# Transformer block in fp32 on one core: the opening rebuilt, weights on a second DMA queue, statistics of batch 0 on VectorE, FFN weight scaling moved into later tiles

## What is computed

```python
def _L0_attn_ref(x, W_qk, W_v, alibi_slope):
    scores = jnp.einsum('bqe,bke->bqk', x @ W_qk, x) * SCALE
    scores = scores + (kpos - qpos) * alibi_slope[0]
    scores = jnp.where(causal, scores, -jnp.inf)
    attn = jax.nn.softmax(scores, axis=-1)
    return jnp.einsum('bqk,bkd->bqd', attn, x @ W_v.T)
def _L0_ffn_ref(x, w_gate, w_up, w_down):   # weights are int32, times 1/127
    h = jax.nn.silu(jnp.einsum('bsd,hd->bsh', x, wg)) * jnp.einsum('bsd,hd->bsh', x, wu)
    return jnp.einsum('bsh,dh->bsd', h, wd)
x = x + _L0_attn_ref(_layernorm(x), W_qk, W_v, alibi_slope)
x = x + _L0_ffn_ref(_layernorm(x), w_gate, w_up, w_down)
```

## Time and profile before

| what | us |
|---|---|
| median of 3 runs | 145.16 (144.49 to 145.37) |
| the profiled execution, whole | 145.67 |
| its span, first to last instruction | 143.9 |
| outside the span (difference) | 1.77 |

### The profile page before, as it was taken

How to read it: one execution, slowest core, us unless ns; L and a number is a source line. 1 busy time by engine, 2 the same in 40 slices (tenths; PEclk the granted TensorE clock), 3 DMA queues, 4 the chain that set the end, 5 groups by cost and what they waited for, 6 DMA issues and landing times.

```text
span 143.9 us, 3450 instructions
## 1 busy us (share of the span) xinstructions
PE 122.8 (85%) x1215; PEld 91.9 (64%) x1215; DVE 120.7 (84%) x341; ACT 110.7 (77%) x251; POOL 97.6 (68%) x157
## 2 busy tenths in 40 slices
PE   0239658999999999999999998979998899999942
PEld 0028345867987769978779776657755656675541
DVE  0729989998697996969996969999879999988781
ACT  4034588999976999949999769985699978999830
POOL 6490769964993454992438943798999999646810
PEclk9999999999999999999999999999999999999995
DMA  4997000000000000000000000000000222022204
GB/s 129 221 244 190 0 0 2 7 2 0 5 0 0 5 0 2 5 0 0 0 5 0 5 0 2 2 5 0 5 0 0 77 77 66 12 73 77 77 0 146
DMA packets 9811, 5.18 MB, mean 36 GB/s; under 512 B 448, under 2 KB 9792, under 8 KB 9792
## 3 DMA queue, kind: packets, MB, share of 16 engines
q1 hardware_dynamic: 9792, 4.92, 12.2%
HBM read 2.82 MB, written 2.10 MB: 34 GB/s over the span
## 4 chain that ended last, share of the span: by engine, by line
PE 50%; DVE 23%; ACT 9%; POOL 7%; DMA 4%; issue 3%; SPq 2%; DVEq 0%
PE work_ps L556 7%; POOL hidden_lo L411 6%; PE attn_ps L571 5%; PE attn_ps L573 4%; PE attn_ps L572 4%; PE score_ps L504 4%; PE score_ps L506 4%; DVE probsT_lo L824 4%; PE score_ps L505 4%; DMA wd_int<-in_L_ffn_w_down_dram 4%; DVE biased L841 3%; PE score_ps L595 2%; PE score_ps L592 2%; DVE stats L726 2%; ACT silu L1069 2%
## 5 line engine op out<-in xcount | busy, mean ns | idle before, releaser
L571 PE MATMUL attn_ps<-v_hi,probsT_hi 128*128 128x128 f16 x144 | 25.8, 219 | 3.0 <-DVE xs L851 2.4
L824 DVE TENSOR_TENSOR probsT_lo<-work_ps,probsT_hi 128x512 f16<-128x512 f32 (+3 forms) x48 | 25.2, 552 | 3.5 <-ACT probsT_hi L1007 3.4
L1007 ACT CAST probsT_hi<-work_ps 128x512 f16<-128x512 f32 (+3 forms) x48 | 21.4, 484 | 7.7 <-PE work_ps L556 7.4
L992 ACT ACTIVATE probs<-biased,neg_max 128x128 f32<-128x128 f32 (+7 forms) x32 | 25.0, 783 | 1.9 <-DVE neg_max L841 1.9
L841 DVE CUSTOM_DVE_ANT_0 biased<-score_ps,bias,neg_score_scale 128x128 f32<-128x128 f32 (+7 forms) x32 | 25.8, 806 | 0.6 <-PE score_ps L506 0.6
L573 PE MATMUL attn_ps<-v_hi,probsT_lo 128*128 128x128 f16 x144 | 25.8, 219 | 0.0
L572 PE MATMUL attn_ps<-v_lo,probsT_hi 128*128 128x128 f16 x144 | 25.8, 219 | 0.0
L556 PE MATMUL work_ps<-ident,probs 128*128 128x128 f32 x144 | 21.4, 274 | 0.2 <-DVE probsT_lo L824 0.2
L411 POOL TENSOR_TENSOR hidden_lo<-hidden,hidden_hi 128x512 f16<-128x512 f32 x13 | 17.6, 1375 | 5.1 <-ACT hidden_hi L1075 5.1
L556 PEld LDWEIGHTS work_ps<-ident,probs 128*128 128x128 f32 x144 | 16.5, 141 | 3.2 <-DVE probsT_lo L824 0.5
L437 POOL TENSOR_TENSOR xT_lo<-whole,xT_hi 128x512 f16<-128x512 f32 x8 | 9.3, 1163 | 13.6 <-ACT whole L986 13.6
(11 more groups left out here) (135 smaller groups left out, 346.7 us busy)
## 6 DMA issues: line engine op xcount, KB each, us to landing
out_dram<-xs SPq DMA_DIRECT2D x7, 256.0 KB, 2.7
xs<-in_L_attn_x_dram SPq DMA_DIRECT2D x3, 512.0 KB, 7.4
xs<-in_L_attn_x_dram SPq DMA_DIRECT2D x2, 256.0 KB, 3.0
out_dram<-xs SPq DMA_DIRECT2D x2, 128.0 KB, 1.9
wgu_int<-in_L_ffn_w_gate_dram SPq DMA_DIRECT2D x1, 192.0 KB, 3.1
wgu_int<-in_L_ffn_w_up_dram SPq DMA_DIRECT2D x1, 192.0 KB, 3.4
wd_int<-in_L_ffn_w_down_dram SPq DMA_DIRECT2D x1, 192.0 KB, 5.1
wqk_in<-in_L_attn_W_qk_dram SPq DMA_DIRECT2D x1, 64.0 KB, 2.9
```

What stands on the lines that cost most here:

```text
L571: pe.matmul(attn_ps[:, 0:D], p_hi, v_j, start=(j == 0), stop=False)
L824: dve.tensor_tensor(probsT_lo[:, i % 2, cols], work_ps[:, bank, 0:n], probsT_hi[:, i % 2, cols], ALU.subtract).then_inc(work_emptied, 1)
L992: act.activation(probs[:, i % 2, 0:n], biased[:, i % 2, 0:n], ACT.Exp, bias=neg_max[:, i:i + 1], scale=-1.0, accum_out=prob_sum[:, i:i + 1 ...
L1007: act.copy(probsT_hi[:, i % 2, CW * h:CW * h + n], work_ps[:, bank, 0:n]).then_inc(probsT_hi_ready, 1)
```

## The change

- **Loads.** The weights and the slope are issued by ACT instead of SP, ahead of everything else on ACT. SP issues batch 0 and then waits for `w_down` before it issues batches 1 to 3. ACT waits for gate and up alone before it casts those.
- **Statistics of batch 0.** POOL's `norm(0)` is gone. DVE takes the attention maxima first, then the statistics, then computes the variances of all eight tiles in seven small steps (`first_variances`); POOL only raises them to the power -0.5, one half at a time; DVE normalises both halves (`normalise_first`).
- **Attention weights.** ACT makes the scaled and high parts, POOL the low ones; DVE did both.
- **Order of the opening.** xT0, q0, xT1, v0, q1, probabilities of tile 0, v1, instead of xT0, xT1, q0, q1, v0, v1, probabilities. PE turns gate and up before xT0 and down after it. The statistics of batch 1 are taken in two groups of four. `norm(1)` on POOL is done half by half.
- **Parts of batch 1**, made during batch 0, move from steps 1 to 6 to steps 3 to 7; for its first halves of xT and q DVE makes the low part from PSUM, and ACT makes no whole copy.
- **FFN weights.** The maxima go to steps 5 and 6 of batch 0 (DVE). The exponents, powers and scales go to steps 1, 2 and 3 of batch 1 (DVE, with a transpose and a spreading matmul on PE in the ring). The scaling goes from ACT to POOL, during batch 2, ahead of `norm(4)`. The high parts go to steps 0 and 1 of batch 3 (ACT), the low parts to POOL in batch 3, ahead of `norm(5)`.

The rest of the diff replaces expressions for indices and counts by a table (`ring`) with the same meaning. The core of the diff:

```diff
+    opening = [("xT", 0), ("q", 0), ("xT", 1), ("v", 0), ("q", 1), ("P", 0), ("v", 1)]
...
+    def parts_at(b, i):
+
+        if b == 0:
+            return {3: [("xT", 0)], 4: [("xT", 1), ("q", 0)], 5: [("q", 1)], 6: [("v", 0)], 7: [("v", 1)]}.get(i, [])
+        return prologue[:HALVES if b == B - 1 else None][i - 1:i] if i else []
...
+    FFN_W = 1
...
+    def by_pool(key):
+
+        return key[0] in ("xT", "q") and (key[1] > 1 or key[1:] == (1, 1))
...
-            sp.dma_start(wqk_in[:, :], w_qk).then_inc(attn_w_loaded, 16)
...
-            sp.dma_start(wgu_int[:, 0:HB, :], w_gate.rearrange("(j p) d -> p j d", p=P)).then_inc(ffn_w_loaded, 16)
...
-            sp.dma_start(wd_int[:, :], w_down).then_inc(ffn_w_loaded, 16)
...
+            sp.wait_ge(wd_loaded, 16)
             for b in range(1, B):
                 sp.dma_start(xs[:, TB * b:TB * (b + 1), :], xv[b]).then_inc(x_loaded[b], 16)
...
-            norm(0)
...
+            first_rstd()
+
+            def attention_weight_low(k):
+                pool.wait_ge(attn_w_scaled, k + 1)
+                pool.wait_ge(attn_w_hi_ready, k + 1)
+                part = (wqk, wvT)[k]
+                pool.tensor_tensor(part[:, 1, :], wtmp[:, k, :], part[:, 0, :], ALU.subtract).then_inc(attn_w_ready, 1)
...
+            attention_weight_low(0)
...
-            norm(1)
...
-            pool.wait_ge(ffn_w_hi_ready, 1)
-            pool.tensor_tensor(wguT[:, 1, :, :], wguT_f[:, :, :], wguT[:, 0, :, :], ALU.subtract).then_inc(ffn_w_ready, 1)
-            pool.tensor_tensor(wdT[:, 1, :, :].rearrange("p a n -> p (a n)"), wdT_f[:, :],
-                               wdT[:, 0, :, :].rearrange("p a n -> p (a n)"), ALU.subtract).then_inc(ffn_w_ready, 1)
...
+            attention_weight_low(1)
+            slopes(slice(0, CW))
+
+            mean_step, var_step = moments(1)
+            for h in range(HALVES):
+                inverse_deviation(1, slice(CT * h, CT * h + CT), var_step)
+                centre(1, h, mean_step)
+                scale(1, h)
...
+            def ffn_weights_scaled():
+                pool.wait_ge(int_scale_ready, 1)
+                pool.wait_ge(ffn_w_copied, 3)
+                for k, w in enumerate((gu_f, d_f)):
+                    pool.tensor_tensor(w, w, int_scale[:, k:k + 1].broadcast_to([P, w.shape[1]]), ALU.mult)\
+                        .then_inc(ffn_w_scaled, 1)
+
+            def ffn_weights_low():
+                for k, (w, hi, lo) in enumerate(((gu_f, gu_hi, gu_lo), (d_f, d_hi, d_lo))):
+                    pool.wait_ge(ffn_w_hi_ready, k + 1)
+                    pool.tensor_tensor(lo, w, hi, ALU.subtract).then_inc(ffn_w_ready, 1)
...
             for b in range(B - 1):
                 nxt = (b + 1) % 2
-                for part in prologue:
-                    if by_pool(part):
-                        split_low(b + 1, nxt, *part)
+                for kind, h in prologue:
+                    if by_pool((kind, b + 1, h)):
+                        split_low(b + 1, nxt, kind, h)
+                if b == FFN_W + 1:
+                    ffn_weights_scaled()
                 norm(b + 2)
             for part in prologue[:HALVES]:
                 split_low(B, B % 2, *part)
+            ffn_weights_low()
             norm(B + 1)
...
+                    if (b, i) == (FFN_W, 1):
+                        pe.wait_ge(w_max_ready, 2)
+                        fill(("wmax", 0, 0), lambda ps: turn_maxima(1, ps))
+                    if (b, i) == (FFN_W, 2):
+                        taken(("wmax", 0, 0))
+                        fill(("wpow", 0, 0), lambda ps: spread_powers(1, ps))
...
+            keep_busy(4)
...
+            spread_powers(0, attn_ps[:, 256:258]).then_inc(w_pow_spread, 1)
+            pe.wait_ge(ffn_w_float, 1)
+            for j in range(2 * HB):
+                m = pe.transpose(gate_up_w_ps[j // HB][:, P * (j % HB):P * (j % HB + 1)], wgu_in[:, j, :], ident[:, :])
+                if j % HB == HB - 1:
+                    m.then_inc(ffn_w_turned, 1)
+            prologue_part(0, 0, "xT", 0)
             pe.wait_ge(ffn_w_float, 2)
-            for j in range(2 * HB):
-                pe.transpose(gate_up_w_ps[j // HB][:, P * (j % HB):P * (j % HB + 1)], wgu_in[:, j, :], ident[:, :])
...
+            keep_busy(2)
             pe.wait_ge(attn_w_ready, 1)
...
+            prologue_part(0, 0, "q", 0)
+            prologue_part(0, 0, "xT", 1)
...
+            pe.wait_ge(attn_w_ready, 2)
+            prologue_part(0, 0, "v", 0)
...
+            def first_variances():
+                stat = stats[:, apart(0), :, :]
+                dve.tensor_tensor(mean_dif[:, :], stat[:, :, 1], stat[:, :, 4], ALU.subtract)
+                dve.tensor_tensor(square_sum[:, :], stat[:, :, 2], stat[:, :, 5], ALU.add)
+                link(dve.tensor_tensor(mean_sum[:, :], stat[:, :, 1], stat[:, :, 4], ALU.add))
+                dve.tensor_tensor(dif_sq[:, :], mean_dif[:, :], mean_dif[:, :], ALU.mult)
+                link(dve.tensor_scalar(within_eps[:, :], square_sum[:, :], 1.0 / D, EPS, ALU.mult, ALU.add))
+                dve.scalar_tensor_tensor(var_eps[:, :], dif_sq[:, :], 0.25, within_eps[:, :], ALU.mult, ALU.add)\
+                   .then_inc(first_var_ready, 1)
+                link(dve.tensor_scalar(mean[:, apart(0), :], mean_sum[:, :], 0.5, None, ALU.mult))
+
+            def normalise_first(h):
+                dve.wait_ge(first_rstd_ready, h + 1)
+                for j in range(CT * h, CT * h + CT):
+                    dve.tensor_scalar(xn[:, j, :], xs[:, j, :], mean[:, 1, j:j + 1], rstd[:, 1, j:j + 1],
+                                      ALU.subtract, ALU.mult).then_inc(first_tokens_ready, 1)
...
+                    if b == FFN_W - 1 and i in (5, 6):
+                        ffn_maxima(i - 5)
+                    if b == FFN_W and i in (1, 2, 3):
+                        (ffn_exponents, ffn_powers, ffn_scales)[i - 1]()
...
-
+                    if b == FFN_W + 2 and i in (0, 1):
+                        ffn_weights_high(i)
...
+            act.dma_start(wqk_in[:, :], w_qk).then_inc(attn_w_loaded, 16)
+            act.dma_start(wv_in[:, :], w_v).then_inc(attn_w_loaded, 16)
+            act.dma_start(wgu_int[:, 0:HB, :], w_gate.rearrange("(j p) d -> p j d", p=P)).then_inc(gu_loaded, 16)
+            act.dma_start(wgu_int[:, HB:2 * HB, :], w_up.rearrange("(j p) d -> p j d", p=P)).then_inc(gu_loaded, 16)
+            act.dma_start(wd_int[:, :], w_down).then_inc(wd_loaded, 16)
...
+            act.wait_ge(gu_loaded, 32)
             act.copy(wgu_in[:, :, :], wgu_int[:, :, :]).then_inc(ffn_w_float, 1)
+            act.wait_ge(wd_loaded, 16)
...
+            def attention_weight(k, source):
+                act.activation(wtmp[:, k, :], source, ACT.Copy, scale=wpow_inv[:, k:k + 1]).then_inc(attn_w_scaled, 1)
+                act.activation((wqk, wvT)[k][:, 0, :], source, ACT.Copy, scale=wpow_inv[:, k:k + 1])\
+                   .then_inc(attn_w_hi_ready, 1)
...
+            def ffn_weights_high(k):
+                act.wait_ge(ffn_w_scaled, k + 1)
+                hi, f = ((gu_hi, gu_f), (d_hi, d_f))[k]
+                act.copy(hi, f).then_inc(ffn_w_hi_ready, 1)
```

522 lines of the change are left out of this document (247 added, 275 removed).

## The result

The changed kernel takes 153.79 us (median of four runs, 152.74 to 154.94) against 144.86 for the kernel before (144.49 to 145.37). The ratio is 1.063, its 95% interval 1.056 to 1.069: it is slower by 6.3%, where I had forecast no measurable difference. The profiled execution has a span of 152.6 us, 8.7 more than that of before.

What follows compares the result with a forecast made beforehand. It took the opening as a chain of waits through the last FFN load, and POOL's list as the path in the last third. Terms -4.3 + 1.3 + 0.4 + 0.1 + 2.8 = +0.3 gave median 145.5 us, range 142.8 to 147.8.

Steps and rivals of the forecast that it cites:

- the opening: Up to DVE's step 0 of batch 0: earlier normalising and less DVE work gain 4.3 us, bounds 3.0 to 5.3.
- batch 0: Added DVE work and a PE stall in step 4 lengthen this batch by 1.3 us, bounds -0.5 to +2.5.
- batch 1: DVE's FFN steps in steps 1 to 3, with 0.45 us of room, add 0.4 us, bounds 0 to 1.2.
- the closing: POOL's FFN low parts ahead of norm(5) push its list, delaying PE's down: +2.8 us, bounds 1.5 to 3.3.
- W_v was put at 3.8: Opening loads: W_v, now second in its queue, was to arrive at about 3.8 us; before, it was awaited until 5.81.
- both hops together: Opening: two hops through PE and ACT for q0 were to show about 1 us more of waiting.
- The stall of PE in step 4: Batch 0: PE was to stand some 2.4 us before batch 1's first scores, awaiting DVE's low part of q0.
- `norm(1)` ends well ahead of its use: POOL's norm of batch 1 was to finish in time, as batch 1's first xT is wanted only in step 3.
- Batch 2: Two FFN scalings on POOL, which runs about 2 us ahead of PE, add 0.1 us, bounds 0 to 0.5.
- My second rival: PE's stall in batch 0, step 4 lowers its clock, costing 1.5 us more: 147.0 us; chance 0.16.
- POOL's list not the path: First rival: POOL's list does not set the closing, which costs 0.6 instead of 2.8 us: 143.3 us; chance 0.27.
- The late second half of the tokens: Third rival: this half lands at 6.8 and delays all variances; opening gains 2.8 us: 147.0 us; chance 0.12.

Runs made afterwards that it cites:

- run 3: Changed kernel with batch 1's parts one per step, steps 2 to 7 of batch 0, instead of two in step 4; 154.06 us, ratio 1.065.
- run 5: Changed kernel with batch 1's statistics ahead of the first scores, its parts in steps 1 to 6, split by POOL; 153.05 us, ratio 1.059.
- run 7: Changed kernel with run 5's order, DVE's FFN work in opening gaps and batch 1 step 5, POOL and ACT FFN work re-placed; 146.81 us, ratio 1.019.
- run 4: Changed kernel with DVE's FFN exponents in step 7 of batch 0, powers and scales in step 7 of batch 1; 154.12 us, ratio 1.064.
- run 1: Changed kernel with POOL's FFN low parts and scalings and ACT's FFN high casts one batch earlier; 149.15 us, ratio 1.030.
- run 6: Kernel before with only POOL's two FFN low parts moved from behind norm(1) to ahead of the closing's norm; 149.65 us, ratio 1.035.
- run 11: Kernel before, unchanged, profiled once more in one execution; 143.98 us.
- run 9: Run 8's kernel with the second half of the first tokens normalised by POOL instead of DVE; 146.08 us, ratio 1.013.
- run 8: Run 7's kernel with POOL's FFN scalings behind norm(2) instead of norm(3); 145.41 us, ratio 1.007.
- run 10: Run 8's kernel with eleven more filling transposes on PE in the opening; 144.04 us, ratio 0.996.

## Why the prediction was wrong

The measured sum is 8.4 us above the forecast one: 2.2 of them lie in the opening, 1.2 in batch 0, 2.0 in batch 1 and 3.1 in the closing. The step that failed most is the closing's: a delay of POOL's list was priced at its own length. Even with every term at its upper bound (-3.0 + 2.5 + 1.2 + 0.5 + 3.3 = 4.5) the forecast would have ended at 149.7 us.

**The opening: -4.3 forecast, -2.1 in the two profiles, -1.0 against the opening that two further executions show.** Three steps failed. First, W_v was put at 3.8 and came at 4.62, which with the small steps makes the first normalising 0.9 us late. Second, the stretch from there to step 0 was to shrink by 1.0 us and grew by 0.4, to 21.87 - 9.66 = 12.21 (11.85 before). I had taken 3.7 us of DVE's work out of it as if DVE alone set its length. From the first normalising to xT's low part DVE needed 12.21 - 9.66 = 2.55 us where before it was 15.52 - 12.12 = 3.40. DVE's work went, but PE's transposes (1.06 us, where they took 0.72 before) and ACT's copy (DVE idle 0.92 before 12.21) took its place, so 0.85 was gained, though some 2.5 us of work had left this part; I had allowed 1.0 for both hops together. From there to step 0 the changed kernel needs 9.66 us and the kernel before 8.45, 1.2 more: the second half's normalising took 1.96 us and not 1.12, beside three spans of POOL. Third, the base: the chain of one execution, whose last load was late, was taken for the program's own, and the wait for that late load was the very thing the change removes.

**Batch 0: +1.3 forecast, +2.5 measured, which is the upper bound that I gave.** The stall of PE in step 4 is there, but 1.82 of its 2.4 us wait for a free bank and only 0.61 for q's low part, so its length is right in part by luck. And the step "`norm(1)` ends well ahead of its use" was wrong in what it left unsaid: it ends in time for the late places only. Runs 3 and 5 show it. As the statistics of batch 1 moved behind the first scores, POOL's norm begins 0.6 us before step 0 (21.25 against 21.87) and not 5.1 (18.89 against 23.97 before), and PE cannot use its waits of steps 0 to 2. An earlier norm gave back 1.1 us; run 7, with the two maxima taken off DVE there as well, gave back the rest and more (19.89).

**Batch 1: +0.4 forecast, +2.4 measured; bounds 0 to 1.2, so outside them.** The term was mis-sized: "Steps 1, 2 and 3 get 0.7, 0.45 and 0.65 us on DVE". They got, from DVE's timeline of the changed kernel, 1.3 (47.81 to 49.11), 0.45 and 1.44 (54.39 to 55.83), since `wpow_diag` took 0.90 us instead of 0.22 and `gu_square` 0.94 instead of 0.16. And the room of 0.45 us in step 1, which I read from a single pair of rows, was no room in steps that are DVE's to begin with: the three steps grew by 1.3, 0.5 and 1.0 us. Run 4 gave back 1.1 of the 2.4; run 7, with almost all of it outside the batch, gave back all.

**Batch 2: +0.1 forecast, 0 measured.** Right; POOL's two scalings are hidden.

**The closing: +2.8 forecast, +5.9 measured.** The mechanism was right, and runs 1 and 6 isolate it: POOL's list is the path, and the work ahead of `norm(5)` moves it all. Measured from DVE's step 7, the norm starts 3.0 us later (97.19 - 104.66 against 91.47 - 101.89), which is my term. Mis-sized is what comes behind, which I had put at nothing. The rows of the kernel before that answer to the later ones are

```profile
110.74 2.73 POOL L411 TENSOR_TENSOR hidden_lo<-hidden,hidden_hi 128x512 f16<-128x512 f32 x2
...
113.53 0.23 PE L688 MATMUL attn_ps<-wdT,hidden_hi 128*128 128x128 f16 x1 [0.44 <-POOL hidden_lo L411]
...
115.08 0.75 DVE L941 SCALAR_TENSOR_TENSOR xs<-attn_ps,ffn_scale,xs 128x512 f32<-128x512 f32 x1
```

and of the changed kernel DVE's add of the same chunk:

```profile
122.91 0.75 DVE L967 SCALAR_TENSOR_TENSOR xs<-attn_ps,ffn_scale,xs 128x512 f32<-128x512 f32 x1 [4.00 <-PE attn_ps L707]
```

POOL's own steps stretch: its first hidden low part starts 4.3 us later (117.81 - 104.66 against 110.74 - 101.89), not 3.0, and `down` of chunk 1 goes 3.8 later. Then PE works at the lower level: from the start of `down` to the add it takes 122.91 - 120.13 = 2.8 us, before 115.08 - 113.53 = 1.55, which is 1.2 more. The add is 5.1 us later. Of the last 0.9 us, 0.2 are lost by the add at 146.88 (138.82 before) and 0.6 between it and the last add, 149.87 - 146.88 = 3.0 us against 141.17 - 138.82 = 2.35. Both kernels have a fallen clock in that stretch (0.71 from 145 to 150, 0.50 from 140 to 144 before); run 11, with 1.00, took 1.8. Run 3 shows the price of the fall behind the wait directly, 1.5 to 1.6 us. My second rival had this price (+1.5 for a fall of the clock), but put it in batch 0, where PE's stalls of 1.8 and 0.6 us did not bring it down. I never asked it of the closing, though I had written that `down` of chunk 1 would wait over 2 us.

**The rivals.** POOL's list not the path (143.3): refuted by runs 1 and 6. The clock in batch 0: right mechanism, wrong place. The late second half of the tokens: refuted by the row at 5.21, though the opening's gain of 2.1 us was even less than the 2.8 of that rival. My range ended at 147.8 because each term was varied alone; the terms of batch 0, batch 1 and the closing had a reason to be worse together, since each put work on an engine that set its stage.

## What to carry to other kernels

Work that leaves an opening is not gone: ask of the place that it goes to which engine sets that stage, and take each added microsecond there at its full length or more; here 2.6 us on POOL cost 3.3 us at best (run 6), 4.7 in run 3 against run 1, and 6.3 in the changed kernel, where the clock fell. Cut both spans at the same instruction of every stage before arguing about causes; here it shows at once that two stages were untouched. And profile the opening of the old kernel twice: it hangs on when loads land, and here two executions of it differed by 1.1 us.

## What the runs showed of the hardware

**DVE and POOL hold each other up.** In the changed kernel, DVE's timeline and POOL's:

```profile
48.29 0.90 DVE L773 TENSOR_SCALAR wpow_diag<-ident,wpow_row 2x2 f32<-2x2 f32 x1
...
54.39 0.94 DVE L816 TENSOR_TENSOR gu_square<-wpow 128x1 f32<-128x1 f32 x1
```

```profile
48.01 1.17 POOL L461 TENSOR_TENSOR xT_lo<-whole,xT_hi 128x512 f16<-128x512 f32 x1 [0.90 <-ACT whole L1012]
...
54.15 1.17 POOL L461 TENSOR_TENSOR qT_lo<-whole,qT_hi 128x512 f16<-128x512 f32 x1 [2.53 <-ACT whole L1012]
```

The first pair ends at 49.19 and 49.18, the second at 55.33 and 55.32. `gu_square` works on one column; it takes 0.16 us in the kernel before. In run 4 it stood beside another POOL span and again ended with it: 64.68 + 0.95 = 65.63 against 63.58 + 2.04 = 65.62; and so did `wpow_diag` there, 44.08 + 0.83 = 44.91 against 42.86 + 2.04 = 44.90. Not held up were a reciprocal of two columns (0.17 us at 64.03 in run 4, inside the same POOL span) and DVE's low parts, which read one operand from PSUM (0.67 us at 50.75 in the changed kernel, inside a POOL span from 50.45 to 51.61). The other way round, POOL's steps of 0.21 us took 0.65 beside DVE's hidden low parts. The Trainium skill says this (SBUF — State Buffer, section "Who interferes with whom"): a DVE instruction with two inputs in SBUF contends with a POOL instruction that reads SBUF, and so does one in a mode that uses both port pairs; there the one that issues first keeps the shared pair to its end, and the other waits in full. The ends above agree with it to 0.01 us (to 0.03 in run 9): in each pair POOL had started first. It costs 0.4 to 0.8 us per small instruction here, which then takes three to six times its length. One row does not fit: in the kernel before `gu_square` took its 0.16 us at 21.31, inside POOL's power step (20.83 to 22.49), and did so again in run 11, so not every POOL span holds DVE up for its whole length. Why that one does not stays open.

**The level of PE's clock in the opening differs between executions of one program.** In the profile of the kernel before, all products of 512 columns take 0.38 us from 16.35 on; in run 11, the same program, they take 0.63 us from 15.48 to 17.6, and 0.38 behind that. Runs 7 and 8, whose openings have the same order, had products of 0.38 us from 13.35 on and of 0.63 us until 24.8, and are 3 us apart at step 0. In run 10, with eleven filling transposes more than run 8, 11 of 12 executions had a span of 141.9 to 143.0 and a granted clock of 1.00. Not tried: such fillers in the kernel before, so how much of the 0.4% is theirs stays open; batch 0, with 0.5 us less, is the only stage in which its profile is ahead of that of run 11, and the two spans, 142.3 and 142.2 us, are alike.
